# One context tile per sequence: heads 0 to 3 and heads 4 to 7 in alternate 16-row halves before the output projection

## The reference

```python
q, k, v = split(layernorm(x).T @ w_in.T + b_in)          # 8 heads of 16
attn = softmax(where(band, q @ k.T / sqrt(16), lowest))
o = (attn @ v) @ w_out.T + b_out                          # 128 -> 128
x = x + (relu(o).T * encodings) mixed by w_ct + b_ct
x = x + routed top-2 experts(layernorm(x)) + shared expert(layernorm(x))
```

## Time and profile before

| | |
|---|---|
| median of 3 runs | 720.66 us (717.82 to 722.0) |
| the profiled execution's own time | 721.22 us |
| its span, first to last instruction | 719.0 us |
| mean granted TensorE clock | 0.966 of full speed |
| busy: TensorE / VectorE / ScalarE / GpSimd | 660.6 / 390.9 / 367.1 / 427.8 us |
| attention stage in steady state | about 90 to 280 us of the span |

### The profile page before, as it was taken

How to read it: one execution, slowest core, us unless ns; L and a number is a source line. 1 busy time by engine, 2 the same in 40 slices (tenths; PEclk the granted TensorE clock), 3 DMA queues, 4 the chain that set the end, 5 groups by cost and what they waited for, 6 DMA issues and landing times.

```text
span 719.0 us, 14013 instructions
## 1 busy us (share of the span) xinstructions
PE 660.6 (92%) x4134; PEld 323.6 (45%) x4134; DVE 390.9 (54%) x1424; ACT 367.1 (51%) x689; POOL 427.8 (60%) x653
## 2 busy tenths in 40 slices
PE   3679899999999999988999999899999989999992
PEld 1345455555555555544445545333333333333330
DVE  3789888888888888851124786322222222222220
ACT  4248667777777767656323222344444344444441
POOL 5248788888888887766110001137767567758763
PEclk8579999999999999999899999999999999999997
DMA  6544544554554433212495943434665566544530
GB/s 211 158 120 114 143 123 130 152 138 133 137 137 137 114 108 102 76 31 79 146 405 189 421 156 120 146 81 99 108 139 128 122 134 123 113 105 83 88 50 0
DMA packets 65275, 95.25 MB, mean 132 GB/s; under 512 B 18345, under 2 KB 43049, under 8 KB 63145
## 3 DMA queue, kind: packets, MB, share of 16 engines
q1 hardware_dynamic: 50544, 66.49, 30.2%
q0 software_dynamic: 9600, 18.89, 14.8%
q10 hardware_dynamic: 5058, 8.99, 3.7%
HBM read 50.99 MB, written 19.14 MB: 98 GB/s over the span
## 4 chain that ended last, share of the span: by engine, by line
PE 67%; DVE 13%; issue 7%; POOL 5%; DMA 4%; ACT 1%; SPq 1%; POOLq 0%; ACTq 0%; DVEq 0%
PE bank L774 18%; PE bank L805 8%; DVE bank L1171 7%; PE bank L600 5%; PE bank L761 4%; PE bank L565 4%; PE bank L793 4%; PE bank L651 4%; PE bank L583 3%; PE bank L754 3%; PE bank L739 3%; PE bank L785 2%; PE bank L659 2%; PE bank L620 2%; PE bank L672 2%
## 5 line engine op out<-in xcount | busy, mean ns | idle before, releaser
L1171 DVE CUSTOM_DVE_ANT_0 bank<-bank,cb 128x192 f32<-128x192 f32 (+1 forms) x512 | 186.0, 418 | 32.8 <-PE bank L565 32.5
L942 ACT ACTIVATE wgu<-bank 128x384 f32<-128x384 f32 (+1 forms) x256 | 125.6, 547 | 45.9 <-PE bank L583 45.4
L774 PE MATMUL bank<-wgu,rowsT 128*64 x320 | 145.9, 599 | 0.0
L776 PE MATMUL bank<-X,rowsT 128*64 128x512 f32 x320 | 145.9, 598 | 0.0
L1404 DVE TENSOR_TENSOR act_in<-act_in,bank 128x256 f32<-128x256 f32 x56 | 23.6, 421 | 201.1 <-ACT act_in L1061 175.7
L565 PE MATMUL bank<-wgu 96*128 96x192 bf16 (+1 forms) x512 | 95.0, 271 | 20.2 <-DVE wgu L1171 14.5
L456 POOL TENSOR_SCALAR_AFFINE_SELECT wgu<-wgu 128x512 f32<-128x512 f32 (+1 forms) x128 | 74.5, 582 | 47.2 <-ACT wgu L942 46.9
L499 POOL DMA_INDIRECT rows<-xn_rows,gather_i x40 | 44.4, 1109 | 88.6 <-DVE gate_of L1399 61.8
L517 POOL DMA_INDIRECT out<-y_out,scatter_i x40 | 65.5, 1638 | 30.6 <-issue 23.0
L517 POOL DMA_INDIRECT out<-y_out,scatter x40 | 58.5, 1462 | 42.0 <-DMA out<-y_out,scatter_i 25.6
L565 PEld LDWEIGHTS bank<-wgu 96*128 96x128 bf16 x512 | 45.2, 101 | 79.9 <-DVE wgu L1171 39.3
(11 more groups left out here) (174 smaller groups left out, 1116.0 us busy)
## 6 DMA issues: line engine op xcount, KB each, us to landing
wgu<-wgu SPq DMA_DIRECT2D x190, 128.0 KB, 2.5
wgu<-w_gu SPq DMA_DIRECT2D x16, 1024.0 KB, 13.1
X<-w_d SPq DMA_DIRECT2D x16, 512.0 KB
out<-y_out ACTq DMA_DIRECT2D x17, 256.0 KB, 3.3
X<-x SPq DMA_DIRECT2D x16, 256.0 KB, 3.3
wgu<-ctx SPq DMA_DIRECT2D x16, 256.0 KB, 3.2
xn_rows<-xn SPq DMA_DIRECT2D x16, 256.0 KB, 2.4
rows<-xn_rows ACTq DMA_DIRECT2D x16, 256.0 KB, 3.5
```

Source lines behind the costliest of these rows:

```text
L774: mm(gb[k.buf][0:GROUP, :], rowsT[:, k.buf, c, 0:GROUP], wgu[:, bass.ds(e * 2048 + 512 * c, 512)], start=(c == 0), stop=(c == 3))
L776: last = mm(gb[k.buf][GROUP:P, :], rowsT[:, k.buf, c, GROUP:P], gu_half[:, k.buf, 512 * c:512 * c + 512], start=(c == 0), stop=(c == 3))
L942: nc.scalar.activation(probs[j % 4][:, 2 * half:2 * half + 2, 0:w], s2[half][:].rearrange("p (j c) -> p j c", j=2)[:, :, 0:w], ACT.Exp, sc ...
L1171: last = v.tensor_tensor_reduce(o, o, cb[:, B_MASK + off:B_MASK + off + w], 1.0, MASKED * 2.0, ALU.add, ALU.max, rowmaxes[n % 2][:, h + i, ...
```

## The change

The values of heads 4 to 7 go into the other 16 columns of `vaug`, so in `ounorm[1]` context and denominators have changed places. A per-partition pair of 0/1 factors (`side`, made once at the start by `find_sides`) picks the rows: ScalarE multiplies `ounorm[0]` by the first (`left_half`, a new activation of 128x512 in unit 1), and VectorE forms `ounorm[1] * side + left` (`join_halves`, new, in unit 2, before the maxima of the second half). One product with the reciprocals (`normalise_out`, in place on the joined tile), one spreading product and one projection are left of two each. The values are copied by two instructions instead of one. Four DMAs on ScalarE's queue (units 4 to 7 of the ramp) put the second half of the weights into the other rows. `residue_q` is moved from unit 4 to the head of unit 5. The projection now carries the waits on `relu_ready` and `m_rows` that the spreading product had.

```diff
@@ -51,6 +51,7 @@
+LEFT = 25
@@ -161,7 +162,8 @@
-        onorm = [over([T]) for _ in range(2)]
+        left = over([T])
+        onorm = over([T])
@@ -174,6 +176,8 @@
+        side = over([2])
+        side_of = over([QB])
@@ -241,8 +245,9 @@
-
-        setup = sem("setup")
+        wo_in = sem("wo_in")
+
+        setup, sides, left_ready, joined = sem("setup"), sem("sides"), sem("left_ready"), sem("joined")
@@ -319,7 +324,8 @@
                 sp.wait_ge(o_copied[g], n + 1)
-                sp.dma_start(dens[64 * g:64 * g + 64, :], ounorm[g][D:P:32, :]).then_inc(dens_in[n % 3], 16)
+                row = D if g == 0 else 0
+                sp.dma_start(dens[64 * g:64 * g + 64, :], ounorm[g][row:P:32, :]).then_inc(dens_in[n % 3], 16)
 
@@ -605,7 +611,7 @@
-                    pe.wait_ge(o_ready, 2 * (n - 5) + 1)
+                    pe.wait_ge(o_ready, n - 4)
@@ -640,17 +646,18 @@
                 after(pe, x2_ready, n)
+                if n == 0:
+                    pe.wait_ge(setup, 7)
+                mm(misc[0][:], cb[0:3 * HEADS, B_SEL:B_SEL + P], recip_rows[0:3 * HEADS, :],
+                   start=True, stop=True).then_inc(den_mm, 1)
+
+            def project_out(n):
                 pe.wait_ge(m_rows, min(n + 3, SEQS))
                 after(pe, relu_ready, n)
-                for g in range(2):
-                    mm(misc[g][:], cb[0:3 * HEADS, B_SEL + P * g:B_SEL + P * g + P], recip_rows[0:3 * HEADS, :],
-                       start=True, stop=True).then_inc(den_mm, 1)
-
-            def project_out(n, g):
-                pe.wait_ge(o_ready, 2 * n + 2)
-                last = mm(misc[1][:], wsm[:, W_O + P * g:W_O + P * g + P], onorm[g], start=(g == 0), stop=(g == 1))
-                if g == 1:
-                    last.then_inc(proj_mm, 1)
+                if n == 0:
+                    pe.wait_ge(wo_in, 16 * QB)
+                pe.wait_ge(o_ready, n + 1)
+                mm(misc[1][:], wsm[:, W_O:W_O + P], onorm, start=True, stop=True).then_inc(proj_mm, 1)
 
@@ -661,7 +668,7 @@
-                pe.wait_ge(o_ready, min(2 * n + 3, 2 * SEQS))
+                pe.wait_ge(o_ready, min(n + 2, SEQS))
@@ -695,9 +702,7 @@
                 if (n := at(U, 28)) is not None:
-                    project_out(n, 0)
-                if (n := at(U, 29)) is not None:
-                    project_out(n, 1)
+                    project_out(n)
                 if (n := at(U, 38)) is not None:
@@ -931,8 +936,9 @@
-                nc.scalar.copy(vaug[n % 3][:, :, :, 0:D].rearrange("p b h d -> p (b h) d"),
-                               misc[0][:].rearrange("p (g d) -> p g d", d=D)).then_inc(v_ready, 1)
+                from_bank = misc[0][:].rearrange("p (b h d) -> p b h d", b=QB, h=HEADS)
+                nc.scalar.copy(vaug[n % 3][:, :, 0:4, 0:D], from_bank[:, :, 0:4, :])
+                nc.scalar.copy(vaug[n % 3][:, :, 4:8, D:2 * D], from_bank[:, :, 4:8, :]).then_inc(v_ready, 1)
@@ -947,8 +953,15 @@
                 act.wait_ge(pv_done, UNITS * n + UNITS - 1 + hg)
-                after(act, o_ready, 2 * n)
+                after(act, joined, n)
                 nc.scalar.copy(ounorm[hg], oacc[hg][:]).then_inc(o_copied[hg], 1)
+
+            def left_half(n):
+                if n == 0:
+                    act.wait_ge(sides, 3)
+                act.wait_ge(o_copied[0], n + 1)
+                after(act, joined, n)
+                nc.scalar.activation(left, ounorm[0], ACT.Copy, scale=side[:, 0:1]).then_inc(left_ready, 1)
 
@@ -983,6 +996,9 @@
                     copy_ones()
+                if 4 <= U < 4 + QB:
+                    i = 32 * (U - 4)
+                    act.dma_start(wsm[i + D:i + 2 * D, W_O:W_O + P], w_small[i:i + D, W_O + P:W_O + 2 * P]).then_inc(wo_in, 16)
                 if U == 3:
@@ -999,6 +1015,8 @@
                     exponentials(*p)
+                if (n := at(U, LEFT)) is not None:
+                    left_half(n)
                 if U == DRAIN - 4:
@@ -1129,7 +1147,8 @@
-                v.memset(vaug[b][:, :, :, D:2 * D], 1.0).then_inc(setup, 1)
+                v.memset(vaug[b][:, :, 0:4, D:2 * D], 1.0)
+                v.memset(vaug[b][:, :, 4:8, 0:D], 1.0).then_inc(setup, 1)
@@ -1184,10 +1203,27 @@
 
-            def normalise_out(n, g):
+            def join_halves(n):
                 after(dve, proj_mm, n)
-                dve.wait_ge(den_mm, 2 * n + g + 1)
-                v.tensor_tensor(onorm[g], ounorm[g], misc[g][:], ALU.mult).then_inc(o_ready, 1)
+                dve.wait_ge(left_ready, n + 1)
+                dve.wait_ge(dens_in[n % 3], 32 * (n // 3 + 1))
+                dve.wait_ge(o_copied[1], n + 1)
+                v.scalar_tensor_tensor(onorm, ounorm[1], side[:, 1:2], left, ALU.mult, ALU.add).then_inc(joined, 1)
+
+            def normalise_out(n):
+                dve.wait_ge(joined, n + 1)
+                dve.wait_ge(den_mm, n + 1)
+                v.tensor_tensor(onorm, onorm, misc[0][:], ALU.mult).then_inc(o_ready, 1)
+
+            def find_sides():
+                dve.wait_ge(setup, 6)
+                halves = lambda cols: cols.rearrange("p (i s d) -> p i s d", i=QB, s=2)[:, :, 1, :]
+                v.tensor_copy(halves(cb[:, B_SEL:B_SEL + P]), halves(cb_f[:, B_SEL + P:B_SEL + 2 * P])).then_inc(setup, 1)
+                v.tensor_reduce(side_of, halves(ident), AX.X, ALU.add).then_inc(sides, 1)
+                dve.wait_ge(sides, 1)
+                v.tensor_reduce(side[:, 1:2], side_of, AX.X, ALU.add).then_inc(sides, 1)
+                dve.wait_ge(sides, 2)
+                v.tensor_scalar(side[:, 0:1], side[:, 1:2], -1.0, 1.0, ALU.mult, ALU.add).then_inc(sides, 1)
 
@@ -1206,12 +1242,14 @@
             def step(U):
+                if (n := at(U, -11)) is not None:
+                    residue_q(n)
                 if (n := at(U, 33)) is not None:
...
                 if (n := at(U, 27)) is not None:
-                    normalise_out(n, 0)
+                    normalise_out(n)
                 if p := piece(U, -1):
@@ -1220,10 +1258,8 @@
                     second_moments(n)
-                if (n := at(U, 27)) is not None:
-                    normalise_out(n, 1)
-                if (n := at(U, -12)) is not None:
-                    residue_q(n)
+                if (n := at(U, 26)) is not None:
+                    join_halves(n)
                 if (n := at(U, -26)) is not None:
@@ -1427,6 +1463,7 @@
+            find_sides()
```

## The result

| | before | changed |
|---|---|---|
| median | 721.24 us (717.82 to 722.0, 4 runs) | 731.12 us (729.72 to 733.18, 4 runs) |
| span of the profiled execution | 719.0 us | 728.3 us |
| mean granted TensorE clock | 0.966 | 0.974 |
| period between additions to x, steady | 19.10 us | 19.92 us |

The account below looks back on a forecast made before the run. The prediction took VectorE and TensorE's chain, with a level second path at unit 6, as the bound. Start +0.9, periods +7.2, tail -3 and 0.6 for the join gave 726.4 us against the median; range of 8 in 10, 716 to 740.

Parts of the forecast that it names:

- What bounds the kernel: Steady period of 19.1 us: 7.4 us of VectorE and 11.7 us of TensorE along the chain.
- A second path ends at unit 6, level with TensorE's own.: Residue, `second_q`, copies and exponentials of unit 5 hold TensorE's shifted scores of unit 6, which already wait 0.08 us.
- the faster rival: TensorE's path alone counts, so the removed 0.88 us comes through in eleven periods: 709 us, chance 0.15.
- What is moved: Residue of q goes behind one more pair of maxima, 0.76 us; `second_q` and the exponentials of unit 5 come 0.6 us later.
- The period: Steady stretch: grows by 0.6 us to 19.7, in 12 periods, +7.2 us; bounds below 0.45, above 0.8.
- its upper bound: Period growth up to 0.8 us, if the first projection of q also waits for the later product in unit 3.
- Start: `find_sides`, four small dependent instructions ahead of the first residue: +0.9 us, bounds 0 and 1.5.
- 0.6 us had been allowed for the join: Added to the sum because the join's bounds (0.66 us taken, 0.60 to 1.82) reach only upward.
- The tail: Last two sequences, one projection, product and spreading product less in each: -3 us, gain between 0 and 5.6.
- the join stands behind GpSimd: Join waits for GpSimd's third part of k, 1.2 us more in VectorE's chain: 744 us, chance 0.13.
- backlog: Unit 2: GpSimd has its own if exponentials came 0.5 us later; the left half was expected hidden in ScalarE's gap.
- The clock as a rival in the steady stretch: TensorE idles about 1.3 us in each unit 6, granted clock falls to 0.60: 744 us, chance 0.07.

Follow-up runs that it names:

- run 9: Kernel before with one output projection per sequence, the context of heads 4 to 7 left out, nothing moved: 718.98 us, ratio 0.9989.
- run 10: Kernel before with only ScalarE's second normalisation put behind the exponentials of unit 4: 719.50 us, ratio 1.0018.
- run 2: Kernel before with only the residue of q moved to the head of unit 5: 729.14 us, ratio 1.0107.
- run 8: Changed kernel with residue back in unit 4, left half in PSUM, second normalisation behind the exponentials of unit 4: 723.78 us, ratio 1.0072.
- run 5: Changed kernel with the residue of q back in unit 4 and the left half written to a PSUM bank: 723.25 us, ratio 1.0053.
- run 6: Changed kernel with only the left half moved to PSUM, residue still in unit 5: 733.12 us, ratio 1.0175.
- run 4: Changed kernel with the residue back in unit 4 and the join early, at the head of unit 0: 722.44 us, ratio 1.0023.
- run 1: Changed kernel with the residue of q back in unit 4, join still in unit 2: 729.05 us, ratio 1.0119.
- run 7: Changed kernel with residue back in unit 4, join early in unit 0, second normalisation behind the exponentials of unit 4: 715.37 us, ratio 0.9935.
- run 3: Changed kernel with left half two units sooner and join at the head of unit 0, residue still in unit 5: 728.38 us, ratio 1.0084.

## Why the prediction was right or wrong

- **What bounds the kernel: right, but for whose path it is.** "A second path ends at unit 6, level with TensorE's own." Runs 9 and 10 show it, and with them that the faster rival was wrong: TensorE's 0.88 us never came through in the steady stretch. But the path that is level is GpSimd's and not the residue's. ScalarE's second normalisation waits for the mean shift, and behind it ScalarE has no gap:

```profile
193.72 0.82 ACT L908 ACTIVATE xn<-X,wgu 128x512 f32<-128x512 f32 x1 [0.30 <-POOL wgu L422]
```

  The residue ended at 194.93, and `second_q` started at 195.18: 0.21 us more than the 0.04 that it needs.
- **What is moved: right to 0.05 us.** The residue went back by 0.76 us, of which its 0.21 us of slack took a part. The move alone gave +0.56 us in each period (run 2) for a forecast of 0.6, with `second_q` 0.39 us idle behind the residue, as was to be seen.
- **The period: a term that was too small.** The forecast was 0.6 us in all, the trace has 0.82. The step that failed is the join in the place of a product, which the sum has as 0.06 us ("194.18 + 0.76 + 0.06"). It takes 0.26 on top of the move, which is the difference between the changed kernel and run 2. The residue starts 9.02 us after the addition, 8.75 in run 2. The join starts 0.07 us later after BN_AGGR than the maxima did there, and takes 0.67 us (200.03 to the next maxima at 200.70) for the product's 0.60. Another 0.10 us is a wait that the text had only in its upper bound, "0.8 (the first projection of q also waits for the later product in unit 3)": that projection starts at 6.17 us in place of 5.40, the scores behind it end at 203.57, and the first maxima of unit 4 start at 203.61, 0.48 us after the ones before them, where 0.38 is the usual distance. These three make 0.24 us:

```profile
203.19 0.38 PE L571 MATMUL bank<-wgu 96*128 96x256 bf16 x2
```

```profile
203.13 0.47 DVE L1190 CUSTOM_DVE_ANT_0 bank<-bank,cb 128x256 f32<-128x256 f32 x1
203.61 0.43 DVE L1190 CUSTOM_DVE_ANT_0 bank<-bank,cb 128x256 f32<-128x256 f32 x1
...
205.11 0.74 DVE L1171 SCALAR_TENSOR_TENSOR wgu<-bank,wgu 128x512 f32<-128x512 f32 x1
```

  With the residue at its old place, the same late projection gives +0.35 over ScalarE's first part of q (run 8).
- **The number of periods.** Twelve at 0.6 us made +7.2. The thirteen distances from the first addition to the fourteenth gave 2.02 + 6.67 + 1.48 = +10.2 us.
- **Start: the term that was furthest off.** The sum had "+0.9 us, bounds 0 and 1.5"; the first addition came 4.47 us late. What was costed is right: the first residue comes at 11.28 in place of 10.28, +1.0. Ahead of it now:

```profile
9.70 0.20 DVE L1221 CAST cb<-wgu 128x64 bf16<-128x64 f32 x1
9.81 0.21 DVE L1222 TENSOR_REDUCE wgu<-cf 128x4 f32<-128x64 f32 x1
10.06 0.16 DVE L1224 TENSOR_REDUCE wgu<-wgu 128x1 f32<-128x4 f32 x1
10.25 0.15 DVE L1226 TENSOR_SCALAR wgu<-wgu 128x1 f32<-128x1 f32 x1
```

  What failed is the step from there to the first addition, which the text put at nothing. Where the other 3.5 us come from stays open. The granted clock fell in places where the kernel before has 1.00. TensorE in stretches of 4 us of the changed kernel (busy, granted clock, DMA share, GB/s; 0.57 is mostly the lower level, 1.2 GHz):

```profile
52.00:56.00 4.00, 3.91 (x30) 0.57 0.57 159
68.00:72.00 4.00, 2.98 (x25) 0.71 0.28 73
...
104.00:108.00 4.00, 2.45 (x17) 0.90 0.02 4
```

  The first two lie ahead of the first addition, the third behind it. But the kernel before has its own, from 16 to 28 and from 36 to 44 us at 0.50, the first of which the changed kernel has not; and run 9 has 1.00 in every such stretch from 8 to 100 us and its first addition at 92.22, 2.5 us after that of the kernel before. So the clock alone is not shown to be the cause. Over the profiled executions the first addition lies between 91.57 and 98.38 us in the nine with `find_sides` and between 87.96 and 93.14 us in the five without it: a part of the loss is likely the change's, and its size is not known.
- **Why the sum came out low.** The periods gave 3.0 us more than forecast, the tail 2.5 us less, and 0.6 us had been allowed for the join: these nearly cancel, by luck. What is left, 9.3 us for 5.7, is the start.
- **The tail: direction right, larger.** -5.5 us for a forecast of -3, just inside its bounds of 0 and 5.6. The last distance is 22.43 us in the changed kernel, 24.76 before and 23.17 with one projection (run 9). The one before it is 15.01 against 18.19 us, but 15.53 in run 2, which has two projections; so that gain is not shown to come from the removed work, and may be the place at which the sequences meet the shared-expert work.
- **The rival "the join stands behind GpSimd": the right contention, the wrong loser.** In the steady stretch the join starts 0.10 us ahead of the third part of k, and it is GpSimd that loses 0.51 us (1.67 for 1.16). With the join's left input in PSUM both keep their length (runs 5 and 6). The Trainium skill ("SBUF — State Buffer", section on who interferes with whom) says that a VectorE instruction with two SBUF inputs contends with a GpSimd instruction that reads SBUF, and that one with a single SBUF input, outside the modes that use two ports, does not. Here the trace agrees with it: 1.67 us with both inputs in SBUF, 1.16 with one in PSUM. In run 4, where the join came onto GpSimd's work, it grew to 1.07 us itself. The cost is less than the rival's 1.2 us, and what it does to the period depends on the path: nothing in the changed kernel (run 6), 0.18 us in each period with the residue back (19.63 against 19.45, runs 1 and 5), 0.86 in those of run 4 that it met.
- **Overlooked: GpSimd's path.** The prediction gave GpSimd a "backlog" and costed it at nothing. It is a path of its own, the one that binds in the kernel before; runs 1 and 4 show it and run 7 takes it out.
- **The clock as a rival in the steady stretch** did not come: 1.00 from 112 to 280 us in the changed kernel, though TensorE idles 0.72 us ahead of the shifted scores of unit 6 in each period. It had fallen just before, to 0.90 and 0.67 in the two stretches from 104 to 112 us, in the period that is 2.02 us longer than before. It came for single periods in runs 3 and 4 (21.0 us).

The sum by what was measured: start and ramp +4.5, periods +10.2, tail -5.5, behind the last addition +0.2, together +9.3 of span, where +0.9, +7.2, -3 and an allowance of 0.6 had been written. Of this the runs show the cause of the periods; that of the start stays open.

## What to carry to other kernels

Where a removed instruction of the busiest engine is worth nothing, look for the point at which several paths meet and time each of them to it: here one start time, that of the exponentials of unit 5, gave the period of all versions with one steady period but one. A change that takes from one path and puts a little on two others loses; with the join out of the way of the product that the projection of q waits for, the residue at its old place and the second normalisation swapped (run 7), the same idea gained 0.65%. When an instruction replaces another "of the same length", ask what was allowed to start after the old one and now waits for the new one too.

## What was not expected of the hardware

- A VectorE instruction of 0.75 us made a GpSimd instruction that started 0.10 us after it 0.51 us longer, somewhat less than the 0.65 us that the two overlap. In run 4 both of a pair grew, the join to 1.07 us and the cast that started 0.48 us after it from 0.20 to 0.66 us.
- TensorE's granted clock fell for single periods of a steady stretch, and the work ahead of the fall does not tell when. In run 3 a stretch of 4 us with 2.88 us of work was followed by one at 0.57 of the full clock, at 1.2 GHz for most of it, and the period took 20.99 in place of 19.2 to 19.7 us; in run 4 the same stretch has 2.83 us of work and the clock behind it stayed at 1.00. The rows of run 3:

```profile
147.00:151.00 4.00, 2.88 (x21) 1.00 0.24 65
151.00:155.00 4.00, 3.95 (x30) 0.57 0.59 169
```
